# A search product moved by one tick into the run of the scores, and a chunk's states summed in one burst in a ring of five banks

## The reference

```
# layer 0, an image
y   = leaky(conv3x3(leaky(conv3x3(x, w1) + b1), w2) + b2)
seq = y as 4096 steps of 64 channels
x, z = split(seq @ in_proj)                      # 128 channels each
x   = silu(conv1d(x, 4 taps, causal) + b)
dt, B, C = split(x @ x_proj)                     # 4, 16, 16
delta = softplus(dt @ dt_proj + b)
h[t] = exp(delta[t] * A) * h[t-1] + (delta[t] * x[t]) * B[t]     # 128 x 16 states
y[t] = sum over the 16 states of h[t] * C[t]
x1  = ((y + D * x) * silu(z)) @ out_proj
# layer 1, an image
out_c = softmax(xc @ xc.T) @ x1                  # channel attention, 64 x 64
q, k, v = 1x1 convolutions of x1                 # 32, 32, 64 channels
out_s = softmax over m of (q[n] . k[m]) @ v      # 4096 x 4096 scores
out = x1 + w_bn @ concat(out_c, out_s)
```

## Time and profile before

| | |
|---|---|
| median of three runs | 9002.96 us |
| profiled execution | 9007.69 us, its span 9005.9 us |
| convolutions | to about 600 us |
| scans without attention | about 640 to 1130 us |
| scans, search and attention | to about 8520 us |
| attention alone at the end | to 9006 us |
| TensorE busy | 8085.0 us (90%) |
| VectorE busy | 7220.5 us (80%) |
| ScalarE busy | 6245.7 us (69%) |
| POOL busy | 3213.1 us (36%) |
| granted TensorE clock, mean | 0.969 |

### The profile page before, as it was taken

The page is one execution under the profiler, slowest core; times in us unless marked ns, Lnnn a source line. Parts: engine busy times, 40 slices in busy tenths (PEclk is TensorE's granted clock), DMA queues, the critical chain, the costliest instruction groups (busy, mean ns, idle before and its releaser), DMA issues. The chain is left out here.

```text
span 9005.9 us, 135283 instructions
## 1 busy us (share of the span) xinstructions
PE 8085.0 (90%) x38865; PEld 2124.9 (24%) x39494; DVE 7220.5 (80%) x10982; ACT 6245.7 (69%) x12374; POOL 3213.1 (36%) x2343
## 2 busy tenths in 40 slices
PE   8962499999999999989999999989999999999999
PEld 2210122222222222222222222222222222222222
DVE  1238989888898888888888889888888988888721
ACT  1124577777777777777777777777777777777754
POOL 0015444343443434333434434333434434333300
PEclk9986699999999999999999999999999999999999
DMA  8758877767677767767776767767777777677500
GB/s 126 117 107 208 205 186 184 184 176 187 179 185 180 192 175 188 183 171 191 178 190 177 191 180 186 181 172 187 183 185 182 188 178 192 175 180 182 148 27 10
DMA packets 868046, 1530.07 MB, mean 170 GB/s; under 512 B 403336, under 2 KB 436944, under 8 KB 867280
## 3 DMA queue, kind: packets, MB, share of 16 engines
q1 hardware_dynamic: 864208, 1520.77, 68.4%
q10 hardware_dynamic: 3072, 0.40, 0.0%
HBM read 1326.69 MB, written 176.95 MB: 167 GB/s over the span
## 5 line engine op out<-in xcount | busy, mean ns | idle before, releaser
L1251 POOL TENSOR_TENSOR hst<-hst,cbc 128x512 f32<-128x512 f32 x2048 | 2844.7, 1390 | 4630.5 <-ACT carry L1007 4005.7
L996 ACT ACTIVATE pr<-bank 128x512 f32<-128x512 f32 x4096 | 2224.9, 597 | 1051.5 <-PE bank L880 950.2
L1144 DVE TENSOR_TENSOR_SCAN hst<-dA,carry,bank 128x512 f32<-128x512 f32 x1792 | 2294.0, 1280 | 64.4 <-DVE bank L1134 0.3
L889 PE MATMUL bank<-pr,vt 128*64 128x512 f32 x8192 | 2212.4, 618 | 0.0
L1086 DVE CUSTOM_DVE_ANT_0 gains<-bank,gains 128x512 f32<-128x512 f32 x2048 | 1406.2, 687 | 855.1 <-ACT gains L944 829.9
L1134 DVE TENSOR_TENSOR bank<-lanes,bbc 128x512 f32<-128x512 f32 x2048 | 1680.3, 820 | 74.2 <-DMA lanes<-spread_d 31.4
L1002 ACT ACTIVATE dA<-lanes,small 128x512 f32<-128x512 f32 x2048 | 1489.4, 727 | 235.6 <-DMA lanes<-spread_d 146.5
L880 PE MATMUL bank<-t2q,t2k 128*128 128x512 bf16 x4096 | 1554.6, 380 | 108.5 <-issue 66.5
L829 PE MATMUL bank<-s1kx,s1q 128*128 128x512 bf16 x4096 | 1337.5, 389 | 286.1 <-DVE mxp L1086 248.2
L878 PE MATMUL bank<-s1q,s1k 128*128 128x512 bf16 x3467 | 1329.4, 383 | 136.0 <-ACT pr L996 135.5
L944 ACT ACTIVATE gains<-bank 128x512 f32<-128x512 f32 x2048 | 1235.6, 603 | 187.0 <-PE bank L829 183.0
(11 more groups left out here) (116 smaller groups left out, 5804.9 us busy)
## 6 DMA issues: line engine op xcount, KB each, us to landing
lanes<-spread_d SPq DMA_DIRECT2D x2048, 512.0 KB, 5.3
seqt<-seq_d SPq DMA_DIRECT2D x256, 128.0 KB, 4.4
spread_d<-dsp SPq DMA_DIRECT2D x128, 256.0 KB, 2.0
spread_d<-usp SPq DMA_DIRECT2D x128, 256.0 KB, 2.0
bbc<-bc_d SPq DMA_DIRECT2D x128, 256.0 KB, 3.3
cbc<-bc_d SPq DMA_DIRECT2D x128, 256.0 KB, 3.8
xpad<-in_x SPq DMA_DIRECT2D x64, 256.0 KB, 6.7
ypad<-ypad SPq DMA_DIRECT2D x128, 128.0 KB, 4.1
```

Source lines behind the costliest of these rows:

```text
L889: mm = nc.tensor.matmul(ACC[CH * h:CH * (h + 1), :], vt[:, t, :], pr[:, T % PRING, h, :], start=t == 0, stop=t == KT - 1)
L996: nc.scalar.activation(pr[:, T % PRING, h, :], bank_of(("S", T, h))[:], ACT.Exp).then_inc(S["p_full"], 1)
L1144: nc.vector.tensor_tensor_scan(hst[:, T % HRING, :], dA[:, T % 2, :], DBU[:], carry[:, g:g + 1] if sl % CHUNKS else 0.0, ALU.mult, ALU.add ...
L1251: nc.gpsimd.tensor_tensor(h, h, cbc[:, (T - 1) // GROUPS % 2, :], ALU.mult).then_inc(S["hc_in"], 1)
```

## The change

The search's second product and its maximum run one tick after the first product and its relu. In a tick TensorE now takes `dif`, the two halves of scores, `max` of the key before, values, sums, small uses. ScalarE takes the relu first in its tick. The sums over the states no longer have a bank: they are a small use `y` in tick 2 of the next chunk, 16 products in one burst, and VectorE reads them at the head of tick 3 and no longer in tick 4. The freed bank goes to the ring, which has five. As POOL's results of a whole chunk have to stay until the burst, `hst` has 24 slots where it had 8: the first half of a chunk's slots alternates between two places. Room for it comes from laying `bcs` into `rest` and `rinv` into `dens`. Three of the four loads of search keys are issued a tick later.

```diff
-SEARCH_LOAD = [SEARCH - KT + 8 * (p + 1) for p in range(QUARTERS - 1)] + [GROUPS]
+SEARCH_LOAD = [SEARCH - KT + 8 * (p + 1) + 1 for p in range(QUARTERS - 1)] + [GROUPS]
-HRING = 8
-BATCH = 4
+HALVES = GROUPS // 2
+HRING = GROUPS + HALVES
...
+def slot_of(T):
+
+    k = T % GROUPS
+    return k if k >= HALVES or T // GROUPS % 2 == 0 else k + GROUPS
...
-        found = self.searches(T)
+        found, last = self.searches(T), self.searches(T - 1)
         if found:
-            t = (T - SEARCH) % KT
-            ev += [("dif", found, t), ("max", found, t)]
+            ev.append(("dif", found, (T - SEARCH) % KT))
+        if last:
+            ev.append(("max", last, (T - 1 - SEARCH) % KT))
...
-        name = {7: "out", 12: "xv", 14: "en"}.get(r)
+        name = {2: "y", 7: "out", 12: "xv", 14: "en"}.get(r)
...
-        uses, plan = self.small_uses(T), []
+        uses = self.small_uses(T)
+        plan = [e for e in uses if e[0] == "dif"]
         if self.attends(T):
             plan += [("S", T, 0), ("S", T, 1)]
+        plan += [e for e in uses if e[0] == "max"]
         if self.attends(T - 1):
             plan.append(("PV", T - 1))
-        plan += uses[0:2]
-        b = T // BATCH - 1
         if T % 2 == 0 and self.attends(T - 1):
             plan.append(("SUM", T // 2 - 1))
-        if T % BATCH == BATCH - 1 and self.scans(BATCH * b):
-            plan.append(("Y", b))
-        return plan + uses[2:]
+        return plan + [e for e in uses if e[0] not in ("dif", "max")]
...
-RING = 4
+RING = 5
...
-    RB, (DBU, ACC, DEN, YPS) = banks[0:RING], banks[RING:]
+    RB, (DBU, ACC, DEN) = banks[0:RING], banks[RING:]
...
-        bcs = sb("bcs", [2 * D_STATE, CHUNK])
+        bcs = rest[0:2 * D_STATE, 0:CHUNK]
-        rinv = sb("rinv", [P, CHUNK])
+        rinv = dens
...
+                        elif kind == "y":
+                            wait(pe, "hc_in", GROUPS * (c + 1) - 1)
+                            for gl in range(GPB):
+                                for j in range(BLOCKS):
+                                    mm = nc.tensor.matmul(
+                                        bank[BLOCK * j:BLOCK * (j + 1), :],
+                                        cst[:, C_SUM + BLOCK * gl:C_SUM + BLOCK * (gl + 1)],
+                                        hst[:, slot_of(GROUPS * c + BLOCKS * gl + j), :],
+                                        start=gl == 0, stop=gl == GPB - 1, tile_position=(0, BLOCK * j))
...
                     for T in range(first, last):
                         sl, r = T // GROUPS, T % GROUPS
+                        near = [e for e in sched.small_uses(T) if e[0] == "dif"]
+                        for e in near:
+                            small_use(e)
                         if sched.attends(T):
...
-                        for e in sched.small_uses(T):
+                        for e in sched.small_uses(T)[len(near):]:
                             small_use(e)
...
-                        if sched.chunk(c) and r == 4:
-                            wait(dve, "y_mm", (GPB * (c + 1) - 1,))
+                        if sched.chunk(c) and r == 3:
+                            full_wait(dve, ("y", c))
                             full_wait(dve, ("out", c - 1))
...
-                            wait(dve, "y_mm", ((T - HRING) // BATCH,))
+                            full_wait(dve, ("y", sl - 1 if T % GROUPS >= HALVES else sl - 2))
```

More of the change, by code:

```diff
@@ L551, in pipeline @@
                    seq0 seq1 lanes0 lanes1 lanes2 lanes3 da_in
-                   dbu_in scan carried hc_in y_mm y_in y2_in st_x1 kd_in head_in rest_in
+                   dbu_in scan carried hc_in y2_in st_x1 kd_in head_in rest_in
                    mid_in low_in st_bc ld_b ld_c abs_in st_split st_vt ring_full act_took dve_took p_full
@@ L627, in span @@
                             sched.note(n, c)
-                for n, offset in (("max_in", TURN - 2), ("nm3_in", TURN), ("nm_row", TURN + 1), ("acc_in", MAIN + KT),
+                for n, offset in (("max_in", TURN - 1), ("nm3_in", TURN), ("nm_row", TURN + 1), ("acc_in", MAIN + KT),
                                   ("den_in", MAIN + KT + 1),
@@ L696, in _ @@
                             wait(sp, "ld_c", c - 2, 16)
-                            issued(sp.dma_start(bc_d[c % 2], bcs[:]), "st_bc")
+                            issued(sp.dma_start(bc_d[c % 2], bcs), "st_bc")
                         if sched.chunk(c) and r == 12:
@@ L905, in sums @@
                         mm.then_inc(S["den"], 1)
-                    def reduce_states(b):
-                        gl = b % GPB
-                        if gl == 0:
-                            wait(pe, "y_in", b // GPB - 1)
-                        wait(pe, "hc_in", BLOCKS * b + BLOCKS - 1)
-                        for j in range(BLOCKS):
-                            mm = nc.tensor.matmul(YPS[BLOCK * j:BLOCK * (j + 1), :],
-                                                  cst[:, C_SUM + BLOCK * gl:C_SUM + BLOCK * (gl + 1)],
-                                                  hst[:, (BLOCKS * b + j) % HRING, :],
-                                                  start=gl == 0, stop=gl == GPB - 1, tile_position=(0, BLOCK * j))
-                        mm.then_inc(S["y_mm"], 1)
                     for T in range(first, last):
@@ L978, in small_use @@
                         elif kind == "BC":
-                            dst, src = bcs[:], bank[0:2 * D_STATE, :]
+                            dst, src = bcs, bank[0:2 * D_STATE, :]
                         elif kind == "out":
@@ L1014, in _ @@
                             wait(act, "den", ((T - 1) // 2 - 1,))
+                            taken(act, ("res", sched.before(done)))
                             nc.scalar.copy(dens[:], DEN[:]).then_inc(S["den_in"], 1)
@@ L1033, in _ @@
                             wait(act, "delta_in", c - 1)
-                            wait(act, "y_in", c - 2)
+                            taken(act, ("y", c - 2))
                             nc.scalar.activation(u[:, c % 2, :], cacc[:], ACT.Tanh).then_inc(S["tanh"], 1)
@@ L1076, in small_use @@
                         kind, c = e[0], e[1]
-                        if kind not in DVE_USES:
+                        if kind not in DVE_USES or kind == "y":
                             return
```

27 lines of the change are left out of this document (12 added, 15 removed).

## The result

The changed kernel takes 9090.11 us (median of 4 runs, 9085.1 to 9101.33) where the kernel before takes 9004.57 beside it: a ratio of 1.0099, 95% interval 1.0081 to 1.0116. It is slower by 86 us; the forecast was 9105.

What follows compares the result with a forecast made beforehand. TensorE led, VectorE close behind, neither full. Per chunk -1.25 - 0.3 + 2.4 = +0.85 us, times 118 = +100; 9007.7 + 100 - 6 + 4 + 5 = 9111, less 5 for the median: about 9105 us, range 8760 to 9280.

Steps and rivals of the forecast that it cites:

- The bound, and the sign: Middle stage: TensorE leads, VectorE close behind, neither full; the change was forecast slower, chance 0.51.
- Products: TensorE's products per chunk: fewer crossings and states in one burst, -1.25 and -0.3 us.
- the bound of -0.4: Limit for the burst's gain per chunk, with all four rows of state products at 0.9 us; -0.3 was taken.
- the crossings: TensorE's switches from bf16 into fp32: some 12.5 ticks a chunk lose one, 0.10 us each, -1.25 us.
- Idle time of TensorE: TensorE's waits per chunk in the middle stage, rising from 3.7 to 6.1 us on the mean: +2.4.
- The chain through ticks 3 to 10: VectorE followed from the burst's end: waits on POOL of 4.65 us, tick 10 ending at 31.6, delaying TensorE's second search product.
- The gauge: Sign the forecast is right: VectorE's product of lanes rises from 820 ns on the mean to over 950.
- The tie of POOL to the maximum: POOL starts some 2.45 us after VectorE's maximum, through relu, exponentials and carry, and so meets VectorE's next product.
- a debt from the burst: VectorE's tick 3 ends at 4.1 us, TensorE's at 2.4; VectorE can't work that off.
- the key loads: Search keys loading against an earlier product: 0 to 2 us an image, 0 to 32 in all, 5 taken.
- The end: Last 122 ticks, search without scans, TensorE alone: every second tick loses a crossing, -6 us, bounds 0 and -12.
- the beginning: First stage, VectorE the bound: ten bursts come up against the start of tick 3, 0 to +20 us, +4 taken.

Runs made afterwards that it cites:

- The cut of POOL's product: POOL's product with C on 64 of 512 columns: in the changed kernel 8588.97 us, in the kernel before 8766.64 us.
- 8745: Changed kernel with ScalarE's carry ahead of the exponentials and VectorE's burst-reading sum just ahead of tick 3's maximum (both moves): 8745.14 us, ratio 0.9709.
- 8938: Changed kernel without the skew: second search product, maximum and relu where they stood before, burst and ring of five kept; 8937.90 us, ratio 0.9925.
- 8947: Kernel before with the skew alone: order, relu and maximum as changed, states in four batches, ring of four; 8947.30 us, ratio 0.9930.
- the kernel of 9046: Changed kernel with the second search product behind the weighted values, where it stood before: 9045.79 us, ratio 1.0046.
- the early carry in the order before: Kernel before with the carry at the head of ScalarE's tick, ahead of the exponentials: 9191.50 us, ratio 1.0203.
- the kernel with three buffers of gains: Changed kernel with three buffers of gains for two, so the relu waits for a maximum one tick older: 8993.91 us, ratio 0.9984.

## Why the forecast came out

**The bound, and the sign: right.** VectorE's wait for the burst is 2.3 us a chunk (2 to 4 were named), the relu's wait has taken the place of VectorE's, POOL starts 2.44 us behind the maximum (2.45), and TensorE's idle time stands before the second search product, released by the maximum. The cut of POOL's product shows the cause: without most of it the change gains 179 us; the forecast's terms without the idle time are (-1.25 - 0.3) x 118 = -183. That these two agree so well is chance, as the terms show.

**The terms, by chunk.** The middle stage went from 62.48 to 63.25 us a chunk, +0.77, where +0.85 was forecast (ticks 256 to 2048, by the starts of the scores). How the parts add up is partly another matter:

- *A gap in the record.* The trace of the kernel before lacks five score products a chunk: the score products that read `s1k` have 4096 weight loads and 3467 products, which belong together one by one. At such a place the next product seems to follow a short stop.

```profile
L878 PE MATMUL bank<-s1q,s1k 128*128 128x512 bf16 x3467 | 1329.4, 383 | 136.0 <-ACT pr L996 135.5 <-DVE mxp L1086 0.5
...
L878 PEld LDWEIGHTS bank<-s1q,s1k 128*128 128x128 bf16 x4096 | 397.1, 97 | 1554.8 <-issue 876.2 <-ACT pr L996 435.3 <-ACT gains L944 18.6
```

```profile
3096.83 0.38 PE L880 MATMUL bank<-t2q,t2k 128*128 128x512 bf16 x1 [0.16 <-issue]
```

  Each time the trace shows 0.05 to 0.16 us of idle time in which TensorE was at work, 0.53 us a chunk in all. The trace of the changed kernel lacks none. So of the 3.7 us of idle time that the forecast started from, some 0.5 were work. The two kernels with POOL's short product lack five a chunk as well, worth 0.53 us (the one made from the kernel before) and 0.29. The figures below are put right by that.
- *Products.* With POOL's product short, TensorE's chunk less its idle time goes from 58.73 to 56.93 us (58.20 and 56.64 by the trace). That is -1.80, or -2.05 at an even clock (last section: 0.42 us a chunk are lost to it in the one, 0.17 in the other), where -1.55 was forecast. The burst has part of the difference:

```profile
3184.63 1.06 PE L917 MATMUL bank<-pr,ones 128*32 128x512 f32 x8
3185.51 3.62 PE L866 MATMUL bank<-hst,cst 128*32 128x512 f32 x32
3189.06 0.39 PE L834 MATMUL bank<-s1kx,s1q 128*128 128x512 bf16 x1
```

  Sums and burst take 4.43 us from start to start, against 5 x 1.00 for the same five rows before: -0.57, not -0.3 (the bound of -0.4 was too near, since the sums in front close up too). That leaves -1.5 for the crossings and what could not be told apart from them, where -1.25 was forecast.
- *Idle time of TensorE.* It rose from 3.5 (4.04 by the trace) to 5.55 us a chunk: +2.05, not +2.4. The chain through ticks 3 to 10 overstated ticks 7 and 8, which lose 0.9 and 0.7, not 1.4 and 2.0. In tick 11 of every other chunk it had 1.2 and the trace has 2.4: not `accs` alone, but `rest` (1.83) and `accs` (1.64) in a row are each held up by POOL.
- *What was missing.* TensorE works slower behind the long stops, up to 0.7 us a chunk (last section). With it -2.05 + 2.05 + 0.7 = +0.7, near the measured 0.77.

So the sum came out in part by luck: the idle term was too long by 0.35, the gain of the products too short by 0.5, and a loss to the clock of up to 0.7 was not in it. The three cancel to within 0.15 us a chunk.

**The gauge was weak.** "Over 950 ns" for the product of lanes came out at 931. But kernels of 8745, 8938 and 8947 us show 916, 911 and 914 ns. The mean tells how long VectorE is held up in all, not what that costs. TensorE's wait for the maximum is no better by itself: 128 us in the kernel of 9046, 186 in that of 8745.

**Step by step.** The tie of POOL to the maximum, which the forecast made the root, is a part of it: untied, 99 us come back, and most of the meetings stay. Shown by runs are a place at which POOL hits the product (the carry moved: -209 us), a debt from the burst (the sum moved: -189), and a bank that TensorE reaches earlier (its wait falls by 306 us when the product stands later, though the time only by 48). Each half of the change alone is faster than the kernel before; that they lose together because they use up the same room is argued from this, and no run takes it apart further. For the key loads the forecast had 5 us, in 0 to 32; the wait for keys became 32.7 us (3.7 before), but removing most of it, in the kernel with both moves, gave 5 us of time. The end gave -4 us (-6), the beginning +6 (+4).

The Trainium skill (SBUF — State Buffer, "SBUF: two separate sides") has the shared port pair as an exclusive lock for a whole instruction. Every run here with POOL's full product agrees: a product of VectorE that comes second ends 0.55 us behind POOL's, however long it had to wait.

## What to carry to other kernels

When two engines exclude one another, look where in the tick each starts, and not only how much each works: one copy of one column, moved ahead of its neighbours, was worth -209 us in one order and cost +182 in another. A burst that saves time on the engine which bounds the kernel makes the engine that reads it late; let the reader do its other work first. Try both halves of a change alone: two gains of 71 and 62 us added up to a loss of 86 here. And where two traces are compared, count the rows first: five that were missing in a chunk looked like half a microsecond of idle time.

## What the runs showed of the hardware

TensorE's clock fell behind stops inside the steady stage, which in the kernel before it does only at the four turns of the loop. In the changed kernel, tick 10 to 11 of a chunk with `accs`: VectorE first, then TensorE, then the busy time by stretch (the third number from the end is the granted clock).

```profile
3722.84 1.83 DVE L1206 TENSOR_TENSOR rest<-x1c,head 64x768 f32<-64x768 f32 x1
3724.70 1.64 DVE L1228 TENSOR_TENSOR accs<-accs,dens 128x512 f32<-128x512 f32 x1
```

```profile
3727.12 0.39 PE L834 MATMUL bank<-s1kx,s1q 128*128 128x512 bf16 x1 [2.43 <-DVE mxp L1089]
3727.44 1.97 PE L903 MATMUL bank<-pr,vt 128*64 128x512 f32 x4
...
3730.18 0.63 PE L894 MATMUL bank<-t2q,t2k 128*128 128x512 bf16 x1
...
3730.94 0.38 PE L894 MATMUL bank<-t2q,t2k 128*128 128x512 bf16 x1
```

```profile
3726.00:3730.00 4.00, 2.88 (x7) 0.67 (x8) 3.93 (x8) 2.88 (x6) 0.49 (x1) 0.68 0.97 257
3730.00:3732.00 2.00, 2.00 (x9) 0.60 (x7) 1.93 (x3) 1.88 (x4) 1.32 (x1) 0.79 0.72 200
3732.00:3734.00 2.00, 2.00 (x16) 0.69 (x13) 1.93 (x5) 0.82 (x3) 1.01 (x1) 1.00 0.84 228
```

After a stop of 2.43 us the weighted values take 1.97 us where they take 1.08 at full clock, and a score product 0.63 where it takes 0.38; the clock goes between its two levels, 2.4 and 1.2 GHz, and stands at 1.00 again in the stretch from 3732 us. From 1600 to 8300 us the changed kernel has 41 such falls besides the loop's turns, each right behind a stop of 2.4 to 2.9 us; the kernel before has no such stop there, and no such fall. In 670 stretches of 10 us from 1600 to 8300 us, (1 - clock) x length adds up to 20 us before and 94 us after the change: up to 74 us, 0.7 a chunk, which no row of idle time shows. In the two kernels with POOL's short product it is 48 us (the changed one) and 19, with both moves 31, and with the early carry in the order before 124. But the kernel with three buffers of gains has 131 us and is faster than the changed one, so it is a share of the loss and not its cause.
